# Moving the shared expert of the last two batches from before the first expert stage to behind it

## The reference, cut to what matters

```python
def _swiglu(xt, wu, wg, wd):
    return jax.nn.silu(xt @ wu.T) * (xt @ wg.T) @ wd.T
logits = xt @ gate_w.T
topk_weight, topk_idx = jax.lax.top_k(jax.nn.softmax(logits, axis=-1), 2)
for e in range(4):
    y = y + combine[:, e:e + 1] * _swiglu(xt, w1[e], w3[e], w2[e])      # routed experts, hidden 512
y = y + _swiglu(xt, sw1, sw3, sw2)                                      # shared expert, hidden 256
...
x = x + _L0_ffn_ref(_layernorm(x), ...)
x = x + _L1_attn_ref(_layernorm(x), ...)                                # RWKV layer
```

## Time and profile before

| what | us |
|---|---|
| median of 3 runs (lowest, highest) | 743.87 (743.05, 746.04) |
| profiled execution, its own time | 742.95 |
| its span, first to last instruction | 741.1 |
| PE busy in the span | 660.9 (89%) |
| DVE busy in the span | 519.2 (70%) |

### The profile page before, as it was taken

One profiled execution on the slowest core, in us unless ns is written; L12 is line 12 of the kernel. 1 busy time (PEld: TensorE's weight loads), 2 busy tenths in 40 slices (PEclk: granted clock), 3 DMA queues, 4 the chain that ended last, 5 costly groups with the idle time before them and its releaser, 6 DMA issues. The chain is left out here.

```text
span 741.1 us, 13768 instructions
## 1 busy us (share of the span) xinstructions
PE 660.9 (89%) x4339; PEld 538.2 (73%) x4339; DVE 519.2 (70%) x1087; ACT 349.6 (47%) x735; POOL 338.2 (46%) x326
## 2 busy tenths in 40 slices
PE   8889999889899999999994799999998589999950
PEld 6656666468788888888883688888887257888840
DVE  6778888957854465444442679999883778888847
ACT  2667777736403333333332365555462654555530
POOL 5977777410033433444213245555442065777530
PEclk9999999989999999999998799999987799999985
DMA  6800000110011311111103942000010012333229
GB/s 205 322 1 3 1 2 15 44 34 29 1 35 44 115 51 58 58 53 57 36 29 108 354 152 98 1 0 1 30 53 33 0 54 81 99 98 101 80 80 309
DMA packets 37186, 54.23 MB, mean 73 GB/s; under 512 B 6645, under 2 KB 28919, under 8 KB 36983
## 3 DMA queue, kind: packets, MB, share of 16 engines
q1 hardware_dynamic: 27832, 31.78, 12.8%
q0 software_dynamic: 7104, 19.41, 8.3%
q10 hardware_dynamic: 2176, 2.10, 0.9%
HBM read 37.28 MB, written 15.99 MB: 72 GB/s over the span
## 5 line engine op out<-in xcount | busy, mean ns | idle before, releaser
L1888 PE MATMUL banks<-r_xt,r_w_mixed 128*128 128x256 f32 x384 | 87.6, 388 | 1.4 <-ACT r_xt L1980 1.4
L1888 PEld LDWEIGHTS banks<-r_xt,r_w_mixed 128*128 128x128 f32 x384 | 73.9, 194 | 12.7 <-ACT r_xt L1980 2.1
L1567 DVE SCALAR_TENSOR_TENSOR f0x_s<-f0x_th,banks 128x512 f32<-128x512 f32 x35 | 24.1, 688 | 83.1 <-ACT f0x_th L1526 83.1
L1427 POOL DMA_INDIRECT f_y<-f0x_yout,f_slot_of x35 | 34.6, 987 | 99.4 <-ACT f0x_yout L1542 99.4
L1413 POOL DMA_INDIRECT f0x_xg<-f_xn,f_token_of x35 | 35.0, 999 | 66.0 <-DVE f_slot_of L1045 49.5
L1526 ACT ACTIVATE f0x_th<-banks 128x512 f32<-128x512 f32 x35 | 21.0, 600 | 86.8 <-PE banks L1478 86.8
L659 DVE TENSOR_REDUCE a_ssum<-a_e 128x6 f32<-128x1536 f32 x32 | 56.0, 1748 | 3.8 <-ACT a_e L526 3.6
L1478 PE MATMUL banks<-f_w_hi,f0x_xt_hi 128*128 x140 | 55.4, 396 | 0.9 <-ACT f0x_xt_hi L1517 0.9
L1478 PE MATMUL banks<-f_w_lo,f0x_xt_hi 128*128 x140 | 55.6, 397 | 0.0
L1413 POOL DMA_INDIRECT f1x_xg<-f_xn,f_token_of x39 | 40.8, 1045 | 32.4 <-DVE f_slot_of L1045 19.3
L1478 PE MATMUL banks<-f_w_hi,f0x_xt_lo 128*128 x140 | 55.2, 394 | 0.0
(11 more groups left out here) (357 smaller groups left out, 1885.4 us busy)
## 6 DMA issues: line engine op xcount, KB each, us to landing
f_w_lo<-in_f_w13T SPq DMA_DIRECT2D x4, 2048.0 KB, 12.0
r_y<-f_y SPq DMA_DIRECT2D x16, 256.0 KB, 5.2
f_w_lo<-in_f_w2T SPq DMA_DIRECT2D x4, 512.0 KB, 15.0
f_xn<-f_rows_normed SPq DMA_DIRECT2D x8, 256.0 KB, 2.1
f_b<-in_f_b SPq DMA_DIRECT2D x1, 2048.0 KB, 9.8
f_w_lo<-in_f_w2T SPq DMA_DIRECT2D x2, 1024.0 KB, 11.6
f_xn<-r_y SPq DMA_DIRECT2D x8, 256.0 KB
f1c_y<-f_y SPq DMA_DIRECT2D x8, 256.0 KB, 7.3
```

Source lines behind the costliest of these rows:

```text
L1427: pool.indirect_dma_start(k.y_dram, bass.IndirectOffsetOnAxis(ap=k.slot_of[:, done:done + 1], axis=0), yout[:, done % YB, :], None).then_i ...
L1567: dve.scalar_tensor_tensor(out=s1[:, t % 2, :], in0=th[:, t % 2, :], scalar=1.0, in1=glu_part, op0=ALU.add, op1=ALU.mult).then_inc(s1_done, 1)
L1888: last = pe.matmul(bank(1 + kind)[:, eb * T:(eb + 1) * T], r.w_mixed[:, kind, j // KB, j % KB, eb * P:(eb + 1) * P], xt[:, b % 2, j % KB, ...
```

## The change

The shared expert of batches 6 and 7 (`LATE = 2`) leaves `first_front`. Its inputs, the turned rows of these batches, and the two weights s13 and s2 now stay in SBUF until the first RWKV block is over. In `rwkv_phase` PE's stream starts with `shared_up` of both batches, with no wait ahead of it. The tanh of batch 6 is put ahead of the first `weigh` on ACT, its gates behind the first `gather_up` on DVE and ahead of `stats(0)`, its `shared_down` behind that; batch 7 follows one batch later, with its `shared_down` between `turn(0)` and `products(0)` on PE. The two additions to x are put behind `stats(2)`. The steps borrow the buffers `rel`, `less` and `ex` of the RWKV block, and PSUM banks 0 to 5. In `first_front` the order of DVE's last steps changes too: the ranking's `experts` and `rows` now come ahead of the fourth addition. POOL's three small memsets, which give `edges`, come ahead of the large one; the wait for `edges` moves on PE to the first `products` and is new on ACT ahead of the first tanh. A constant is half as wide.

```diff
 def first_front(nc, m, v, k, ctx, block):
...
-        for c in range(2, B - 1):
+        for c in range(2, FRONT - 1):
             up(c + 1)
             if c == 2:
                 rank.count(pe)
-            elif c == 4:
+            elif c == FRONT - 2:
                 rank.list(pe)
             down(c)
-        down(B - 1)
+        down(FRONT - 1)
...
         steps.tables()
         gated(5)
-        add(4)
         steps.experts()
         steps.rows()
         take_low(dve, 10)
-        gated(6)
+        take_low(dve, 11)
+        add(4)
+        steps.weigh()
         add(5)
-        steps.weigh()
-        take_low(dve, 11)
-        gated(7)
-        add(6)
-        add(7)
...
     def schedule(w):
...
+        for z in range(LATE):
+            w.shared_up(z)
+        w.shared_tanh(0)
         w.weigh(0)
         w.gather_up(0)
+        w.shared_gate(0)
+        w.shared_down(0)
         w.stats(0)
         w.root(0)
         w.weigh(1)
+        w.shared_tanh(1)
         w.gather_up(1)
+        w.shared_gate(1)
         w.stats(1)
         w.norm(0)
         front(0)
+        w.shared_down(1)
         w.weigh(2)
         w.root(1)
         w.norm(1)
         w.gather_up(2)
         w.products(0)
         w.stats(2)
+        for z in range(LATE):
+            w.shared_add(z)
...
+            def shared_up(self, z):
+                shared_up(pe, k, s_banks(z), k.turned(B - LATE + z)).then_inc(done["shared_up"], 1)
+
+            def shared_down(self, z):
+                pe.wait_ge(done["shared_h"], z + 1)
+                shared_down(pe, k, s_result(z), s_h(z)).then_inc(done["shared_down"], 1)
...
             def products(self, b):
                 pe.wait_ge(done["xt_ready"], b + 1)
+                if b == 0:
+                    pe.wait_ge(done["edges"], 1)
...
-        pe.wait_ge(done["edges"], 1)
         schedule(PE())
...
+            def shared_tanh(self, z):
+                if z == 0:
+                    act.wait_ge(done["edges"], 1)
+                act.wait_ge(done["shared_up"], z + 1)
+                act.activation(s_th(z), s_banks(z)[0], ACT.Tanh, scale=first.slope / 2).then_inc(done["shared_th"], 1)
...
-        pool.memset(f32(later.b2[:]), 0.0).then_inc(bias_zero, 1)
-        pool.memset(spare[:], 0.0).then_inc(done["spare_zero"], 1)
         pool.memset(xt[:, :, :, 0], 0.0)
         pool.memset(top[:, :, 0], NEVER)
         pool.memset(ab[:, :, :, 0], 0.0).then_inc(done["edges"], 1)
+        pool.memset(f32(later.b2[:]), 0.0).then_inc(bias_zero, 1)
+        pool.memset(spare[:], 0.0).then_inc(done["spare_zero"], 1)
```

More of the change, by code:

```diff
@@ L815 @@
 EARLY = 4
+LATE = 2
 def gate_products(pe, m, k, b):
@@ L822, in gate_products @@
         for kb in range(KB):
-            last = pe.matmul(m.banks[:, 1, at:at + k.experts], k.xt[:, b, kb, s * P:(s + 1) * P], k.gate[:, kb, :],
+            last = pe.matmul(m.banks[:, 1, at:at + k.experts], k.turned(b)[:, kb, s * P:(s + 1) * P], k.gate[:, kb, :],
                              start=(kb == 0), stop=(kb == KB - 1))
@@ L1057, in weigh, with shared_up, shared_down @@
         then(dve.tensor_tensor(weight[:, 1, :], t.ex2[:], weight[:, 0, :], ALU.mult))
+def shared_up(pe, k, banks, turned):
+    HS = k.shared_hidden
+    for j, bank in enumerate(banks):
+        for hb in range(HS // P):
+            col = j * HS + hb * P
+            for kb in range(KB):
+                last = pe.matmul(bank[:, hb * S * P:(hb + 1) * S * P], k.s13[:, kb, col:col + P], turned[:, kb, :],
+                                 start=(kb == 0), stop=(kb == KB - 1))
+    return last
+def shared_down(pe, k, result, h):
+    HSB = k.shared_hidden // P
+    for s in range(S):
+        for hb in range(HSB):
+            last = pe.matmul(result[:, s * D:(s + 1) * D], h[:, hb * S * P + s * P:hb * S * P + (s + 1) * P],
+                             k.s2[:, hb, :], start=(hb == 0), stop=(hb == HSB - 1))
+    return last
 def first_front(nc, m, v, k, ctx, block):
@@ L1113, in up @@
             at_least(pe, h_done, c - 1)
[L1114 to L1120, removed]
+            shared_up(pe, k, (glu(c), lin(c)), k.turned(c)).then_inc(up_done, 1)
         def down(c):
@@ L1124, in down @@
             at_least(pe, added, c)
[L1125 to L1129, removed]
+            shared_down(pe, k, result, h[:, c % 2]).then_inc(down_done, 1)
         up(0)
@@ L1191, in _ @@
         rank.negate(act)
-        for c in range(5, B):
+        for c in range(5, FRONT):
             tanh(c)
@@ L1678, in rwkv_memory, with rwkv_phase @@
     return r
-def rwkv_phase(nc, m, r, k, ctx, block, A, v, later):
+def rwkv_phase(nc, m, r, k, ctx, block, A, first, v, later):
     EB = KB
@@ L1708, in rwkv_phase @@
              "out_done x_done bn_done aggr_done eps_done next_rstd next_mean "
-             "late_xn late_in late_xt late_logits spare_zero late_stored")
+             "late_xn late_in late_xt late_logits spare_zero late_stored "
+             "shared_up shared_th shared_s1 shared_h shared_down shared_added")
     done = {n: sem(n) for n in names.split()}
@@ L1718, in rwkv_phase @@
     late_bank = lambda c: bank(2 * (c % 2))
+    s_banks = lambda z: (bank(2 * z), bank(2 * z + 1))
+    s_result = lambda z: bank(4 + z)
+    s_th, s_s1, s_h = (lambda z: flat(rel[:, z])), (lambda z: flat(less[:, z])), (lambda z: flat(ex[:, z]))
     def schedule(w):
@@ L1805, in rwkv_phase, with shared_up, shared_tanh, shared_gate @@
     class Work:
+        def shared_up(self, z): pass
+        def shared_tanh(self, z): pass
+        def shared_gate(self, z): pass
+        def shared_down(self, z): pass
+        def shared_add(self, z): pass
         def weigh(self, b): pass
@@ L2042, in _, with shared_gate, shared_add @@
         class Dve(Work):
+            def shared_gate(self, z):
+                dve.wait_ge(done["shared_th"], z + 1)
+                dve.scalar_tensor_tensor(out=s_s1(z), in0=s_th(z), scalar=1.0, in1=s_banks(z)[0], op0=ALU.add,
+                                         op1=ALU.mult).then_inc(done["shared_s1"], 1)
+                dve.wait_ge(done["shared_s1"], z + 1)
+                dve.scalar_tensor_tensor(out=s_h(z), in0=s_s1(z), scalar=0.5, in1=s_banks(z)[1], op0=ALU.mult,
+                                         op1=ALU.mult).then_inc(done["shared_h"], 1)
+            def shared_add(self, z):
+                b = B - LATE + z
+                two = m.x_res[:, S * b:S * b + S, :]
+                dve.wait_ge(done["shared_down"], z + 1)
+                dve.tensor_tensor(two, two, s_result(z).rearrange("p (s c) -> p s c", s=S), ALU.add).then_inc(done["shared_added"], 1)
             def stats(self, b):
@@ L2265, in first_layer @@
         later.weights = [None, weight_part(nc, later_v, "lo", kept, "right")]
-        rwkv_phase(nc, m, r, k, scope, block, later_inputs, later_v, later)
+        rwkv_phase(nc, m, r, k, scope, block, later_inputs, v, later_v, later)
     return later
```

25 lines of the change are left out of this document (15 added, 10 removed).

## The result

| | median us (lowest, highest; runs) | against before |
|---|---|---|
| before, beside it | 743.46 (742.48, 746.04; 4) | |
| changed | 733.94 (731.65, 734.18; 4) | 0.9861, 95% interval 0.9835 to 0.9886 |
| changed, on a second chip | 732.20 (730.88, 734.14; 5) | 0.9859 (0.9833 to 0.9884) |
| changed, on a third chip | 732.43 (731.86, 733.76; 5) | 0.9860 (0.9840 to 0.9879) |

A forecast was written before the change was run, and what follows sets the result against it. PE was taken to bound three stretches, with a 12.8 us hole between the last two. Gains 10.4 + 0.1 + 0.1 = 10.6 took the profiled 742.95 to 732.3, median about 733.0; range 729.5 to 737.5.

The forecast's parts named there:

- The front: End of first front: two `up` and two `down` leave PE, so `up(0)` starts 10.4 us earlier, bounds 9.4 to 10.8.
- two chains: End of first front: after the move, either PE's own `down` queue or the gathers' chain is late next.
- The first gather: End of first front: the gather still takes 2.06 us, now beside two `take_low` in a row.
- The RWKV block: Start of RWKV block: clock gain of 0.2 less 0.1 for POOL and DVE, net gain 0.1 us.
- DVE, ACT and POOL: Start of RWKV block: moved steps fit idle time; 0.1 us deducted for POOL and DVE together.
- The constant: Very start of the kernel: the narrower constant halves a memset, gaining 0.1 us, bounds 0 and 0.3.
- The bounds: First front: gain at least 9.4 us if the second gather lands 1 us late or one `down` runs at low clock.
- the forecast's own range: Whole kernel: the main forecast, given chance 0.62, spans 731.8 to 735 us.
- (a): Start of RWKV block: PE's clock holds at 2.4 GHz; total gain 12.3, time 731.5 us; chance 0.20.
- (b): Front gain halves because gathers set the turn, or RWKV steps cost 4 us; about 737.5 us; chance 0.13.
- (c): Start of RWKV block: `shared_up` is held and the moved block delays the chain; slower, up to 749 us; chance 0.03.
- (d): Whole kernel: work only moves from one place on PE's path to another; no change, 743.9 us; chance 0.02.

The follow-up runs named there:

- the two orders: The changed kernel with the old order on DVE, 739.05 us; the kernel before with the new order alone, 742.38 us.
- The last experiment: The changed kernel plus constant matmuls nobody reads on PE, around the front's list and before the first RWKV turn: 729.39 us, ratio 0.9824.
- both repeats: The changed kernel run again unaltered on the second and third chips: 732.20 and 732.43 us.
- the filled hole: The changed kernel plus six constant matmuls on PE between `shared_down(0)` and the first RWKV turn: 732.62 us, ratio 0.9843.

## Why the prediction was right

The median came out 0.9 above the 733.0 forecast, and below it on the two other chips.

**The front: predicted 10.4, measured 10.48.** Each step holds against the start of the list: first gather 4.57 us behind it predicted, 4.64 measured; turn 9.7 to 9.9 and 9.66; `up(0)` 11.27 and 11.17. That two chains are late at once, PE's and the gathers', was the step that mattered, and the two orders show it: the 11.0 us of PE alone bring 4.5, the order alone nothing. The forecast lets `down(4)` at the low clock and then the addition set `down(5)`. So it is: the addition waits 0.29 us for `down(4)`, and `down(5)` waited 0.87 and not 1.09. The last experiment shows how little was behind it: with `down(4)` at the full clock, 1.3 us faster, the front gains only 0.3, since both `take_low` stand ahead of that addition.

**The first gather: 2.06 kept, 2.06 measured.** It took 2.06 beside one `take_low` (before, and the kernels with one batch moved) and beside two, and 1.23 in the kernel in which DVE was idle beside it. The one row without it puts the cost of the two-input DVE operation at 0.8 us, whether one stands there or two. The Trainium skill, page "SBUF — State Buffer", section "Who interferes with whom", names this contention, and the runs agree with it. No gather was held until both operations had ended. A hold until the end of the first one is not excluded: the gather ended 1.10 us behind that end in the kernel before (215.58 and 214.48), in the changed one (209.08 and 207.98), and with one batch moved (209.07 and 207.97).

**The RWKV block: predicted 0.1, measured 0.24, and 0.7 in both repeats.** The net is near, and its two parts are right in kind. The products start 17.04 us behind the last tile instead of 14.60, 2.4 more, and take 2.70 less. I had 1.2 and about 1.4: I let `shared_down(1)` run at the full clock (1.89) and the products be partly slow. Measured, `shared_down(1)` took all of the low stretch, 3.35, and the products none. Both terms were short by about the same, 1.2 and 1.3, and the sum stood: that is luck. That the idleness just ahead of the turn (3.06 us, 2.66 and 2.58 in the repeats), and not the hole of 12.8, brings the clock down is shown by the filled hole, in which it stays at 1.00. The Trainium skill, page "TensorE: Matmul & The Clock Gate", section "HAM oscillation — how this bites in real kernels", has PE put back to the low clock while it waits for a DMA, and each burst behind such a wait start cold; the page makes this depend on how long PE waits, which the prediction left out. Here `shared_down(0)` behind 1.19 us ran at 1.00 (1.99 us). Behind the longer waits the clock did fall, but into the burst and not ahead of it: in the third trace the turn ran at 1.00 behind 2.58 us, and the 3.1 us behind the turn at 0.54.

**DVE, ACT and POOL: 0.1 predicted, nothing measured.** From the end of the last tile to the first turn every kernel takes 12.7 to 12.9 us, with the steps (12.71 and 12.69 in the repeats), without them (12.87) and before (12.82); only the profiled execution of the changed kernel shows 13.14. There the second plane came 0.4 us later: ACT's first `weigh`, which waits for that DMA, starts 7.04 us behind the last tile, against 6.64 before and 6.62 and 6.61 in the repeats. It was this landing, and not one of the moved steps, that came late.

**The constant: predicted 0.1, and not shown.** The list came 1.15 earlier in the profiled execution, but PE's granted clock was low at another place (0.91 from 20 to 60 us before, 1.00 after, 0.96 in the second trace), and in the repeats the list starts at 202.88 and 203.76. I take the 1.15 for the clock; nothing here tells 0.1 us apart.

**The bounds.** 9.4 was too high a floor for the front. I had allowed for one `down` at the low clock; with both there, as in the kernel without the moved steps, the front gives 8.2. With it the forecast's own range would have reached 1.2 higher. The term that was too small is the price of a slow `down`: the 3.30 of the kernel before was low for a part only, and one that is low throughout takes 3.75, not 1.4 but 1.9 more than 1.89.

**The rivals.** (a), the clock held, did not occur. The filled hole shows what it is worth: last tile to second turn falls from 27.66 before to 25.26, 2.4 us, where (a) had 1.9. (b) occurs when the order on DVE is left as it was: there the gathers set the turn, 739.05. (c) did not occur: `shared_up` starts at the end of the last tile. (d) is excluded.

## What to carry to other kernels

When work is taken off the engine that bounds a stretch, ask which chain is late next, and move it ahead of any instruction that waits: here the ranking stood behind a waiting addition, and without moving it more than half of the gain was lost. Work put into a hole is free if each of its steps lands in measured idle time, and it may pay by keeping the clock; but here the clock fell again behind the 2.6 to 3.1 us of idleness that were left just ahead of the burst that matters. An edit worth 1 or 2 us is judged between marks of the trace in repeats, since the median of a few runs moves as much by itself.

## What the runs showed of the hardware

The same instructions at the same place ran at either clock in different kernels and runs: `down(4)` behind the list took 1.96, 3.26, 3.36 and 3.74 us. Every profile has some short stretches at a low clock, and these do not all repeat. The time of one kernel goes with its mean granted clock: the five runs of the second chip have 730.88, 731.12, 732.20, 733.36 and 734.14 us at 0.955, 0.955, 0.952, 0.950 and 0.948. It is no exact rule (on the third chip 731.86 us stands at 0.950 and 732.41 at 0.952), only one of these runs has a trace, and between kernels it fails, since PE's idle time counts too: 733.62 us without the moved steps stands at 0.936. I had not expected that most of a kernel's spread, 3.3 us here, goes with this, nor that it hides a gain of 1.7 us that its stage shows plainly.
